# One-core fused network (attention, deformable convolution, attention, scan block): the spreading matmuls read 32 rows in place of 128

## The reference

```
for each tap k:
    W_k[(i,j), q] = mask * hat(y_k(q) - i) * hat(x_k(q) - j)     # 256 source pixels x 256 output pixels
    out[o, q]    += sum over (i,j) of (dcn_w_k x)[o, (i,j)] * W_k[(i,j), q]
```

## Time and profile before

| | |
|---|---|
| median of three runs | 418.3 us |
| lowest and highest run | 414.33 and 418.74 us |
| profiled execution, first to last instruction (its own time is not given beside it) | 416.3 us |
| TensorE, VectorE, ScalarE, GpSimd busy | 355.3, 286.1, 205.2, 107.6 us |
| TensorE's granted clock, mean of the span | 0.904 |

### The profile page before, as it was taken

One profiled execution on the slowest core, in us unless ns is written; L12 is line 12 of the kernel. 1 busy time (PEld: TensorE's weight loads), 2 busy tenths in 40 slices (PEclk: granted clock), 3 DMA queues, 4 the chain that ended last, 5 costly groups with the idle time before them and its releaser, 6 DMA issues.

```text
span 416.3 us, 6350 instructions
## 1 busy us (share of the span) xinstructions
PE 355.3 (85%) x2060; PEld 192.6 (46%) x2060; DVE 286.1 (69%) x623; ACT 205.2 (49%) x463; POOL 107.6 (26%) x178
## 2 busy tenths in 40 slices
PE   3759989998899989999899989999899988944613
PEld 2643545645455553645464554555464434324301
DVE  2226535595965878496978697596858698877681
ACT  1163365367416672477537652576337653543512
POOL 0130220140413231330424140422223141142241
PEclk9979999999869996899999986999689999997655
DMA  7000000000000000000000000000000000000000
GB/s 236 14 0 2 14 2 2 13 2 0 2 1 2 1 28 0 2 1 25 0 0 0 27 0 0 0 0 25 0 0 0 13 1 0 2 13 0 0 13 13
DMA packets 3042, 4.66 MB, mean 11 GB/s; under 512 B 336, under 2 KB 2768, under 8 KB 2896
## 3 DMA queue, kind: packets, MB, share of 16 engines
q1 hardware_dynamic: 3024, 4.43, 3.3%
HBM read 3.38 MB, written 1.05 MB: 11 GB/s over the span
## 4 chain that ended last, share of the span: by engine, by line
PE 52%; DVE 29%; issue 9%; ACT 6%; POOL 1%; DMA 1%; DVEq 0%; ACTq 0%; SPq 0%; POOLq 0%
PE ps_cv L497 13%; DVE sb_acc L992 10%; DVE sb_wt L933 5%; DVE sb_dw_acc L978 5%; PE ps_yb L481 5%; PE ps_ma L421 5%; PE ps_mb L568 4%; PE ps_mb L542 3%; PE ps_xb L478 3%; PE ps_mb L528 3%; PE ps_wx L465 2%; PE ps_mc L590 2%; ACT sb_xe L717 2%; PE ps_ma L412 2%; PE ps_ma L450 2%
## 5 line engine op out<-in xcount | busy, mean ns | idle before, releaser
L933 DVE TENSOR_TENSOR sb_wt<-ps_yb,sb_xe 128x512 f32<-128x512 f32 x144 | 97.2, 685 | 65.4 <-ACT sb_xe L717 49.2
L497 PE MATMUL ps_cv<-sb_wt,sb_w_x 128*64 128x256 f32 x576 | 100.0, 428 | 0.0
L481 PE MATMUL ps_yb<-sb_hats,sb_sel 128*128 128x512 f16 x144 | 57.6, 409 | 3.9 <-DVE sb_wt L933 3.7
L497 PEld LDWEIGHTS ps_cv<-sb_wt,sb_w_x 128*64 128x64 f32 x576 | 29.8, 141 | 55.3 <-issue 49.8
L992 DVE SCALAR_TENSOR_TENSOR sb_acc<-sb_y_pad,sb_par,sb_acc 128x256 f32<-128x256 f32 x96 | 52.1, 596 | 2.5 <-ACT sb_acc L788 2.4
L717 ACT ACTIVATE sb_xe<-ps_xb 128x512 f32<-128x512 f32 x72 | 43.0, 597 | 9.4 <-PE ps_xb L478 9.4
L1115 POOL TENSOR_TENSOR sb_acc<-sb_acc,sb_g_tmp 128x256 f32<-128x256 f32 x32 | 24.9, 779 | 63.2 <-ACT sb_acc L788 59.6
L978 DVE SCALAR_TENSOR_TENSOR sb_dw_acc<-sb_z_pad,sb_par,sb_dw_acc 128x256 f32<-128x256 f32 x56 | 36.7, 704 | 3.2 <-ACT sb_dw_acc L773 3.1
L465 PE MATMUL ps_wx<-sb_par,sb_x 128*128 128x256 f32 (+1 forms) x144 | 36.6, 376 | 0.4 <-ACT sb_w_x L708 0.4
L1075 POOL TENSOR_TENSOR sb_dist<-sb_pos,sb_par 128x1152 f32<-128x1152 f32 (+1 forms) x8 | 16.7, 2089 | 71.4 <-DVE sb_pos L886 71.4
L743 ACT ACTIVATE sb_b_exp<-ps_mb,sb_b_neg 128x256 f32<-128x256 f32 x28 | 13.0, 470 | 41.7 <-DVE sb_b_neg L943 41.7
(11 more groups left out here) (172 smaller groups left out, 547.4 us busy)
## 6 DMA issues: line engine op xcount, KB each, us to landing
sb_par<-in_par SPq DMA_DIRECT2D x1, 1339.5 KB, 8.5
sb_x_in<-in_x SPq DMA_DIRECT2D x8, 128.0 KB, 2.1
out_y<-sb_y_out SPq DMA_DIRECT2D x8, 128.0 KB, 1.7
sb_par<-in_par SPq DMA_DIRECT2D x1, 397.0 KB, 4.6
sb_sel<-in_sel SPq DMA_DIRECT2D x1, 224.0 KB, 4.7
sb_par<-in_par SPq DMA_DIRECT2D x1, 192.0 KB, 2.7
sb_par<-in_par SPq DMA_DIRECT2D x1, 128.0 KB, 2.2
```

The lines of the kernel that those rows point to most:

```text
L481: nc.tensor.matmul(yb[h][:, :], sel_sb[:, P * (3 + 2 * odd + h):P * (4 + 2 * odd + h)], hats[:, g, :], start=True, stop=True).then_inc(ev( ...
L497: mm = nc.tensor.matmul(cv[C * b:C * (b + 1), 0:PIX], w_x[:, h, k, C * b:C * (b + 1)], wt[k % 2][h][:, PIX * b:PIX * (b + 1)], start=(s == ...
L933: nc.vector.tensor_tensor(wt[k % 2][h][:, :], yb[h][:, :], xe[k % 2][:, :], ALU.mult)\
```

## The change

The matmuls of `spread` take 32 rows of `sel_sb` and `hats` in place of 128: those of the slot that they need. `y` is rows 0 to 31 for an even tap and 64 to 95 for an odd one, `xx` is rows 32 to 63 or 96 to 127. The rows left out meet zeros in `sel_sb`, so that the result is the same. Columns, outputs, waits and order stay as they are.

```diff
                 k, h = divmod(s, 2)
                 g, odd = divmod(k, 2)
+                y = slice(2 * SLOT * odd, 2 * SLOT * odd + SLOT)
+                xx = slice(2 * SLOT * odd + SLOT, 2 * SLOT * (odd + 1))
                 if h == 0:
                     if k % 4 == 0:
                         pe.wait_ge(ev(f"hats_ok{k // 4}"), n)
                     wait_past(pe, ev("xe_ok"), tap(n, k - 1))
-                    nc.tensor.matmul(xb[:, :], sel_sb[:, P * (1 + odd):P * (2 + odd)], hats[:, g, :],
+                    nc.tensor.matmul(xb[:, :], sel_sb[xx, P * (1 + odd):P * (2 + odd)], hats[xx, g, :],
                                      start=True, stop=True).then_inc(ev("xb_mm"), 1)
                 wait_past(pe, ev("wt_ok"), slot(n, s - 2))
-                nc.tensor.matmul(yb[h][:, :], sel_sb[:, P * (3 + 2 * odd + h):P * (4 + 2 * odd + h)], hats[:, g, :],
+                nc.tensor.matmul(yb[h][:, :], sel_sb[y, P * (3 + 2 * odd + h):P * (4 + 2 * odd + h)], hats[y, g, :],
                                  start=True, stop=True).then_inc(ev("yb_mm"), 1)
```

## The result

The changed kernel is slower: median 427.55 us against 418.35, ratio 1.0224 with a 95% interval of 1.017 to 1.0278, so that it is slower by more than the noise, but not surely by 2%. The profiled execution took 427.42 us, with a span of 425.6 us; a run lies 1.8 us above its span. Executions more than 1.5% above the fastest of their kernel are left out of every ratio in this document: here the one of 439.33 us, with a mean granted clock of 0.832 against 0.87 in the other three.

The account below looks back on a forecast made before the run. TensorE and VectorE take turns on the chain (52% and 29% of the span), with TensorE's clock counting; 416.3 - 5.4 + 4.6 + 8.5 + 6.3 + 2.3 + 4.0 = 436.6, plus 2.0, rounded to 438 us; range 414 to 452.

Parts of the forecast that it names:

- the last passage: Passage with spreads from 332.17 us, fast before: a fall and a longer slow stretch there, 4.6 + 1.7 = 6.3 us lost.
- the second pair's: Passage from 62.10 us, fast before: a fall there costs 4.6 us, counted half, 2.3 us.
- the start: First pair's spreads, where the low clock must come back: slow for 8 us longer, 4 us lost (bounds 0 and 10).
- 5.4 us of gain: TensorE's chain, whole kernel: 8.1 us saved by 29 overlapping pairs, less 2.7 us for 30 layout switches.
- The pair overlaps: Even slots: `xb` and first `yb` matmul run side by side on different rows, saving 0.22 us, 0.43 at slow clock.
- The switch: A 32-row spread behind a full-array matmul switches the array's layout, about 0.09 us each, 2.7 us in all.
- One more fall in the passage that kept its clock: Passage from 195.53 to 238.00 us: its clock now falls too, 47.11 - 42.47 = 4.6 us lost.
- Longer slow stretches: Five passages of the loop: slow stretches of 10.2 us become a third longer, 1.7 us each, 8.5 us in all.
- rival A: Faster: pairs overlap and rows do not matter to the clock, 412.9 us; chance 0.17.
- rival C: Much slower: the clock, once low, stays low through a whole dense stretch, 458 us; chance 0.06.
- the step of the rows: TensorE's clock: matmuls on part of the array's rows keep it up less than full ones; the step trusted least.
- plain reading: Clock gate follows busy time, not rows: falls stay where they are, time is the first rival's, 412.9 us.

Follow-up runs that it names:

- filled kernels: The kernel before and the changed kernel, each with six unread full-array matmuls added in slot 2 of each pass from the third on: 399.07 and 405.56 us.
- filled changed kernel: The changed kernel plus six unread matmuls on all 128 rows in slot 2 of each pass from the third on: 405.56 us, ratio 0.9759.
- filled kernel before: The kernel before plus six unread matmuls on all 128 rows in slot 2 of each pass from the third on: 399.07 us; run again, 399.96 us.
- small extra matmuls: Six unread matmuls on 32 rows and 32 columns added in slot 2: on the kernel before 401.78 us, on the changed kernel 420.02 us.

## Why the prediction was wrong

The direction held, the loss is the clock's, and the time lay in the range, but the change cost 9.2 us and not the 19.7 I forecast. The step that failed is the pricing of slow time that no row showed: the last passage, the second pair's and the start were put at 12.6 us and measured 1.7. Two more terms were off and nearly cancelled, which was luck: the 13.1 us of clock in the loop (4.6 + 8.5) came to 8.2, and the 5.4 us of gain to 0.9 between filled kernels. By its steps:

- **The pair overlaps** as put: 0.23 us became 3 ns. **The switch** as put: behind `wx` the spread starts at 0.31 us in place of 0.21. What failed besides is the step from there to the end of the kernel: the sum took the 29 pairs and 30 switches of the chain before as all the time won and lost, -5.4 us. Between filled kernels, in which no clock disturbs, a passage went from 42.45 to 42.38 us only, the third pair's from 42.80 to 42.59, the second's from 38.93 to 38.68, the last from 34.12 to 34.01: 0.9 us in all. The chain of such a passage shows where the win goes. Of the filled changed kernel:

```profile
197.97 0.32 PE ps_xb L465
198.29 0.00 PE ps_yb L468
...
206.66 0.32 PE ps_xb L465
206.98 0.00 PE ps_yb L468
206.98 0.58 PE ps_cv L484 x4
207.56 0.11 issue
207.68 0.69 PE ps_mc L565 x2
```

and of the filled kernel before, at the same places:

```profile
190.91 0.21 PE ps_xb L463
191.13 0.22 PE ps_yb L466
...
199.71 0.32 PE ps_xb L463
200.03 0.22 PE ps_yb L466
200.25 0.58 PE ps_cv L482 x4
200.83 0.63 PE ps_mc L563 x2
```

  The passage has four pairs on its chain, and each gives up its 0.22 us: 0.87 in all. But six spreads, each the first behind other work, take about 0.32 us in place of 0.21 to 0.23, as at 197.97 against 190.91: 0.6 us back. Behind one pair TensorE stands 0.11 us before `fuse`, which needs VectorE's `o_sum`; that ends at 207.54 (its instruction starts at 207.12 and takes 0.42), and `fuse` takes 0.06 more. What is left, 0.07 us, arrives at the end of the passage. For the passage from 195.53 the sum had counted three pairs and four switches, 0.3 us. It left out a spread that pays as well, the one behind `attn_t` (0.32 in place of 0.23), and the wait before `fuse`; and with the filling two more spreads lie on the chain. For a passage with a fall it had counted 0.7 us, two of the pairs at 0.43, and there came 0.2 (47.11 to 46.91): the slow stretch is 10.2 us long in both, so that work done sooner in it only lets later work into it. The `wx` chunk behind `fuse` takes 1.71 us there (at 168.90) in place of 0.86 (at 169.10).
- **One more fall in the passage that kept its clock**: forecast 4.6 + 1.7 us (the 1.7 from the next term), measured 48.31 - 42.47 = 5.8. Right, though a fall more or less also occurs between executions of one kernel.
- **Longer slow stretches**, forecast 1.7 us in each of five passages: it came in three of five, where the passages grew by 1.0 us (47.39 to 48.40, 47.08 to 48.10); two passages kept 10.2 us and became 0.2 us shorter. With the net gain of 0.2 taken out, a longer stretch costs 1.2 us, not 1.7; its length, a third more than 10.2, came as guessed. The term was 8.5, and 3 x 1.2 = 3.6 came.
- **The last passage**, forecast 6.3 us, measured 35.49 - 34.18 = 1.3: the fall came late there, at 353 us, and lasted 6.5 us.
- **The second pair's passage**, forecast 2.3 us: no fall, 38.68 against 38.93.
- **The start**, forecast 4.0 us, measured 62.68 - 62.10 = 0.6. The filled changed kernel lost 7.6 us there, so the bound of 10 was not idle.
- Together: 0.6 - 0.25 + 1.0 - 0.2 + 5.8 + 1.0 - 0.2 + 1.3, and 0.2 for the end, is 9.3 us, the difference of the spans (425.6 - 416.3).

So of the terms that rested on rows of a fall one was right and one too large (8.5 us, measured 3.6), and those that I set for falls that no row showed (last passage, second pair, start: 12.6 us) measured 1.7. Against rival A: what the narrow spreads do to the array matters for the clock, as the first pair shows at equal work. Against rival C: the clock did come back in every dense stretch of the loop; at the start it took until 48 and 51 us in two kernels.

The ground on which the step of the rows stood was weak. It compared the stretch before the fall at 158.7, with its 64-row logits, with one late in the kernel. The passage that kept its clock, the nearest one to compare with, has the same logits at the same place, no fall came behind them, and the prediction doesn't show them:

```profile
L528 PE MATMUL ps_mb<-sb_k,sb_q 64*128 64x256 f32 x4 | 1.1, 395 | 0.7 <-ACT sb_v L760 0.7
```

(window 203.1 to 206.5 of the kernel before). That the step came out right in kind was luck as far as this comparison goes; it is the experiments that show it.

The plain reading of the Trainium skill's page TensorE: Matmul & The Clock Gate, Part 1, that the gate follows how busy the engine is, does not cover the 22.8 us at 1.2 GHz with the engine busy for 22.69. Its Part 3 has matmuls of different row groups start some 4 ns apart; the trace agrees, with 3 ns.

What stays open is what exactly makes the clock fall. Every kernel with fewer rows also has more switches of the array's layout, and no run has one without the other. Idle moments at the switches are hardly enough by themselves: the 14 spreads from 28.5 to 51.3 us would make some 1.4 us of them at 0.1 each (an estimate), while TensorE kept 2.4 GHz with 3.52 us busy of 5 in the earlier trace rows. But a switch may count in another way, so "rows" in this document means rows with the switches that they bring. The share of the array alone is not it (the small extra matmuls did prevent falls with 128-row spreads), nor the working time alone (they did not with 32-row ones). That falls come and go by one between executions of one kernel, 412.4 or 418 us for the kernel before, makes counts of falls in single profiles weak; the verdicts rest on the medians.

## What to carry to other kernels

Cutting the unused rows off a matmul saved no time on it: 0.31 us to the next start with 32 rows as with 128. It let neighbours on other rows overlap, 0.22 us a pair, but the switch to another layout gave 0.1 us back at each spread behind full-width work, and a wait for another engine took 0.17 of what was left: count both before you count the overlap as time won. And it makes TensorE's work thinner, which can cost clock, 4.6 to 5.8 us for each slow stretch here. In a kernel that hands over between TensorE and another engine, look first at the granted clock passage by passage; a few unread matmuls in the idle gaps before a dense stretch were worth 4% here, 14 to 18 us against the 0.9 us that the rows gave at best.

## What I had not expected of the hardware

- In one profiled execution TensorE stayed at 1.2 GHz for 22.8 us while busy for 22.69 of them, with a part of its matmuls on 32 rows; with 128 rows in these it had 2.4 GHz after 32 us.
- Six matmuls of 512 columns on 32 rows and 32 columns, 1.3 us in a passage of 42 us (6 x 0.21), stood against a median of 412.97 us before and 401.78 after; in the profiled execution every passage of the loop had 2.4 GHz.
- The first pair's instructions, the same and on the same 32 rows, had the clock back at 35 us in one kernel and at 51 in another, so one profile doesn't give the size of a loss by the clock.
